# A scan's skip term as a diagonal matrix product, with its reader on another engine

## The reference, cut to what matters

```python
xc = silu(conv(x_ssm) + conv_b)                      # 4 x 512 x 256
dt = softplus(dt_r @ dt_proj_w.T + dt_proj_b)
dA = exp(dt[..., None] * A)
dBx = dt[..., None] * Bv[:, :, None, :] * xc[..., None]
h = dA_t * h + dBx_t                                 # for each step t
y = einsum('bdn,bn->bd', h, C_t)
y = ys + xc * D                                      # the skip term
return y * silu(z) @ out_proj_w.T
```

## Time and profile before

| | |
|---|---|
| median of 3 runs | 1700.42 us (1700.09 to 1701.14) |
| profiled execution | 1702.22 us |
| its span, first to last instruction | 1700.4 us |
| TensorE matmul busy | 1603.6 us (94%) |
| VectorE busy | 1213.6 us (71%) |
| ScalarE busy | 1046.0 us (62%) |
| GpSimd busy | 1014.2 us (60%) |
| mean granted clock of TensorE | 0.981 |

### The profile page before, as it was taken

How to read it: one execution, slowest core, us unless ns; L and a number is a source line. 1 busy time by engine, 2 the same in 40 slices (tenths; PEclk the granted TensorE clock), 3 DMA queues, 4 the chain that set the end, 5 groups by cost and what they waited for, 6 DMA issues and landing times.

```text
span 1700.4 us, 24061 instructions
## 1 busy us (share of the span) xinstructions
PE 1603.6 (94%) x7156; PEld 1225.9 (72%) x7156; DVE 1213.6 (71%) x2082; ACT 1046.0 (62%) x2093; POOL 1014.2 (60%) x976
## 2 busy tenths in 40 slices
PE   8999788788899999999899999998999999999998
PEld 6777444344577767877788778887887778878886
DVE  4565798889756656896678468876784588756665
ACT  4344867666443466676678666665785666656665
POOL 1100667767410068987333589883435788878887
PEclk8999899989999999999999999999999999999999
DMA  2000000000000066665000256652002567656664
GB/s 107 24 0 0 1 1 1 0 1 1 26 1 1 1 177 160 173 163 145 23 1 1 73 144 176 172 136 58 1 1 55 146 159 173 156 151 172 170 174 105
DMA packets 57829, 137.36 MB, mean 81 GB/s; under 512 B 10267, under 2 KB 33267, under 8 KB 57331
## 3 DMA queue, kind: packets, MB, share of 16 engines
q1 hardware_dynamic: 57715, 135.99, 31.0%
HBM read 133.86 MB, written 2.10 MB: 80 GB/s over the span
## 4 chain that ended last, share of the span: by engine, by line
PE 74%; POOL 8%; ACT 7%; issue 5%; DVE 3%; PEld 1%; PEldq 1%; POOLq 1%; DMA 0%; SPq 0%; ACTq 0%; DVEq 0%
PE ps L228 22%; PE ps L229 21%; PE ps L230 21%; POOL ln_c L1180 6%; PE ps L1706 2%; PE ps L905 1%; PE ps L1691 1%; PE ps L1692 1%; PE ps L1693 1%; POOL e_lo L236 1%; PE ps L371 1%; PEldq L217 1%; ACT ln_t L1017 1%; ACT L1017 1%; PE ps L377 1%
## 5 line engine op out<-in xcount | busy, mean ns | idle before, releaser
L236 POOL TENSOR_TENSOR e_lo<-e_h,e_hi 128x512 fp32r<-128x512 f32 (+1 forms) x368 | 476.6, 1295 | 128.2 <-ACT e_hi L233 117.4
L1356 ACT ACTIVATE e_s<-ps 128x512 f32<-128x512 f32 (+1 forms) x368 | 220.1, 598 | 267.8 <-PE ps L230 267.0
L1512 DVE TENSOR_TENSOR ps<-e_s,ps 128x512 f32<-128x512 f32 x352 | 244.8, 695 | 185.4 <-PE ps L230 150.6
L228 PE MATMUL ps<-xn_hi,eh 128*128 128x512 f32 x704 | 283.3, 402 | 9.1 <-ACT e_s L1356 7.4
L229 PE MATMUL ps<-xn_lo,eh 128*128 128x512 f32 x704 | 280.0, 398 | 0.0
L230 PE MATMUL ps<-xn_hi,el 128*128 128x512 f32 x704 | 279.3, 397 | 0.0
L1517 DVE TENSOR_TENSOR e_h<-ps,rwb 128x512 f32<-128x512 f32 x352 | 243.4, 691 | 14.8 <-DVE ps L1512 2.2
L236 POOL TENSOR_TENSOR el<-e_raw,eh 128x128 fp32r<-128x128 f32 (+1 forms) x352 | 219.8, 624 | 23.5 <-ACT eh L1345 23.5
L233 ACT ACTIVATE e_hi<-e_h 128x512 fp32r<-128x512 f32 (+1 forms) x368 | 229.5, 624 | 6.6 <-DVE e_h L1517 6.5
L1180 POOL TENSOR_TENSOR ln_c<-m_h,m_c 128x512 f32<-128x512 f32 x128 | 168.5, 1322 | 78.7 <-DVE m_h L1125 71.0
L228 PEld LDWEIGHTS ps<-xn_hi,eh 128*128 128x128 f32 x704 | 132.4, 188 | 49.5 <-ACT e_s L1356 10.0
(11 more groups left out here) (273 smaller groups left out, 3277.5 us busy)
## 6 DMA issues: line engine op xcount, KB each, us to landing
e_raw<-in_experts SPq DMA_DIRECT2D x176, 192.0 KB, 3.9
rwb<-rw_rows SPq DMA_DIRECT2D x64, 352.0 KB
rwb<-rw_rows SPq DMA_DIRECT2D x80, 256.0 KB
rwb<-rw_rows SPq DMA_DIRECT2D x32, 320.0 KB
rwb<-rw_rows SPq DMA_DIRECT2D x48, 192.0 KB
rwb<-rw_rows SPq DMA_DIRECT2D x32, 224.0 KB
rwb<-rw_rows SPq DMA_DIRECT2D x32, 160.0 KB
rwb<-rw_rows SPq DMA_DIRECT2D x80, 64.0 KB
```

What stands on the lines that cost most here:

```text
L228: pe.matmul(out, w_hi, x_hi, start=start, stop=False, skip_group_check=True)
L236: return eng.tensor_tensor(lo, full, hi.bitcast(F32), ALU.subtract)
L1356: act.activation(e_s[0:rows_, buf, :], ps[0:rows_, 4, :], ACT.Silu).then_inc(S["silu"], 1)
L1512: dve.tensor_tensor(ps[:, bank, :], e_s[:, buf, :], ps[:, 5, :], ALU.mult).then_inc(S["gated"], 1)
```

## The change

The skip term becomes a product on TensorE, with a diagonal matrix of D that VectorE makes once. It is the first of the sum, ahead of the identity product of state 0, so that one starts the bank and the other accumulates. VectorE's two additions are gone; ScalarE copies the sums from PSUM to `m_y` in `finish` of items 5 and 6. The steps that follow (gating, high and low part, output product, add) and those that use bank 6 after them come one item later.

```diff
+                skip_d = fb("skip_d", [P, MC, P])
...
-            for q in range(12):
+            for q in range(13):
                 finish(NB - 1, q)
...
-                    if q == 13:
+                    if q == 14:
                         ...
                         bc_proj(i + 1, FREE_BANK)
-                    if q == 17:
+                    if q == 18:
                         ...
                         dt_proj(i + 1, FREE_BANK)
...
                 if n == 0:
                     after(pe, "ylin", 2 * i + m - 1)
+                    pe.wait_ge(*M("skip_set", MC))
+                    pe.wait_ge(*M("xc", 2 * i + m + 1))
+                    pe.matmul(ps[:, 4 + m, :], skip_d[:, m, :], xc[:, i % 3, m, :], start=True, stop=False, skip_group_check=True)
                 pe.wait_ge(*M("hc", 32 * i + q + 1))
-                pe.matmul(ps[:, 4 + m, :], ident, m_hc[:, q % DEEP, :], start=(n == 0), stop=(n == DS - 1),
+                pe.matmul(ps[:, 4 + m, :], ident, m_hc[:, q % DEEP, :], start=False, stop=(n == DS - 1),
...
             def finish(i, q):                       # TensorE
-                if q == 9:
+                if q == 10:
...
-                    if q == 17:
+                    if q == 18:
                         bc_high(i + 1, FREE_BANK)
...
             def finish(i, q):                       # ScalarE
+                if q in (5, 6):
+                    m = q - 5
+                    act.wait_ge(*M("y_sum", 32 * i + 31 + m))
+                    after(act, "g_lo", 2 * i - 1 + m)
+                    act.activation(m_y[:, m, :], ps[:, 4 + m, :], ACT.Identity).then_inc(M["ylin"], 1)
-                if q == 9:
+                if q == 10:
...
+            for m in range(MC):                     # VectorE, once
+                dve.tensor_scalar(skip_d[:, m, :], ident, cols[:, C_D + m:C_D + m + 1], None, ALU.mult).then_inc(M["skip_set"], 1)
...
-                    if q == 16:
+                    if q == 17:
                         bc_low(i + 1, FREE_BANK)
...
             def finish(i, q):                       # VectorE
-                if q == 1:
-                    for m in range(MC):
-                        dve.wait_ge(*M("y_sum", 32 * i + 31 + m))
-                        dve.scalar_tensor_tensor(m_y[:, m, :], xc[:, i % 3, m, :], cols[:, C_D + m:C_D + m + 1], ps[:, 4 + m, :],
-                                                 ALU.mult, ALU.add).then_inc(M["ylin"], 1)
...
-                if q == 11:
+                if q == 12:
                     dve.wait_ge(*M("out", i + 1))
...
             def finish(i, q):                       # GpSimd
-                    if q in (2, 3):
+                    if q in (3, 4):
...
-                    if q in (7, 8):
+                    if q in (8, 9):
```

More of the change, by code:

```diff
@@ L207, in program @@
             "bcproj dtproj bc_hi bc_lo v vabs e ln dt du b_spread c_spread da db h c_copy hc y_sum ylin "
-            "gated g_hi g_lo out x_new aexp bc_zero").split(), 0), 1)
+            "skip_set gated g_hi g_lo out x_new aexp bc_zero").split(), 0), 1)
         A, = group("att", dict.fromkeys((
@@ L1193, in finish @@
                 if i < NB - 1:
-                    if q in (2, 3):
-                        m = q - 2
+                    if q in (3, 4):
+                        m = q - 3
                         pool.wait_ge(*M("sz", 2 * i + 2))
@@ L1198, in finish @@
                         pool.tensor_tensor(m_y[:, m, :], m_y[:, m, :], sz[:, i % 3, m, :], ALU.mult).then_inc(M["gated"], 1)
-                    if q in (7, 8):
-                        m = q - 7
+                    if q in (8, 9):
+                        m = q - 8
                         pool.wait_ge(*M("g_hi", 2 * i + m + 1))
```

## The result

The changed kernel takes 1705.78 us (median of 8 runs, 1704.39 to 1707.95), the kernel before 1699.72 (8 runs, 1695.16 to 1701.14): ratio 1.0037, 95% interval 1.0027 to 1.0047. It is slower, by some 6.1 us. Its profiled execution took 1707.95 us (span 1705.6, mean granted clock 0.980), 5.7 more than the one of before; each of the two is the slowest of its eight. Run again beside the last experiments (E9) it gave 1.0035 (1.0024 to 1.0045), with a second profiled execution of 1705.74 us.

What follows compares the result with a forecast made beforehand. VectorE was taken to set the scan phase's pace. Terms 0.4 + 2.0 + 2.0 - 0.6 + 1.3 - 0.65 = +4.45 took 1700.42 to 1704.9 us, range 1698.5 to 1708.5.

Steps and rivals of the forecast that it cites:

- The late read: Starts of blocks 1 to 3: TensorE waits 3.5, 3.5 and 2.75 us for ScalarE's read, queued behind the copy of C.
- Gain against new wait: Starts of blocks 1 and 2: 1.29 us saved by removed additions, against 1.4 us wait for spread 5 at full clock.
- full-clock replay: Starts of blocks 1 and 2 without half clock: spread 5 at 255.3, spread 6 at 258.0, nothing gained or lost.
- The half clock: TensorE at 1.2 GHz behind the new wait: +2.0 us each in blocks 1 and 2, bounds 0 and +2.5.
- block 3: Its start: new TensorE wait of 2.75 us, -0.1 at full clock, 0.7 to 1.7 later at half; taken as +1.3.
- rival B: Half clock behind the new wait in two of three blocks: about 1.9 us less, 1703.0; chance 0.20.
- six of six waits: All six earlier waits for the copy of C of 2.55 us or more went with TensorE at half speed.
- The moved steps: Output product and other steps one item later: -0.3 us in each of blocks 1 and 2, bounds 0 and -2.9.
- Rival D: Full clock at block starts and behind the shorter wait ahead of the output product: -6.15, 1694.3; chance 0.08.
- Block 0: Skip products add 1.7 to 2.6 us ahead of spread 6, against 1.31 cover: +0.4, bounds 0 and +1.3.
- The tail: End of the phase: with ScalarE reading instead of VectorE's second addition, the second gating ends earlier, -0.65 us.

Runs made afterwards that it cites:

- E9: The changed kernel run once more, nothing altered, against the kernel before; 1704.35 us, ratio 1.0035.
- E1: Changed kernel, but ScalarE reads the two sums in items 3 and 4 instead of 5 and 6; 1699.67 us, ratio 0.9996 to the kernel before.
- E4 short: Changed kernel plus 11 calls (22 small useless matmuls) on TensorE ahead of the wait for ScalarE's read, blocks 1 and 2; 1702.11 us, 1.0007 to before.
- E3: Changed kernel without the skip product (D * xc left out of the result), ScalarE still reading late; 1699.42 us, ratio 0.9997 to the kernel before.
- E2: Kernel before, VectorE's additions kept and no skip product, but the later steps one item later as in the change; 1699.38 us, ratio 1.0000.
- E5: Changed kernel with ScalarE reading in items 3 and 4 and later steps in their old items, skip product first; 1697.27 us, 0.9993 to before.
- E7: Kernel before with only ScalarE's reads in items 3 and 4 and the skip product ahead of products 6 and 7; 1693.41 us, 0.9961, again 0.9976.
- E8: Changed kernel with the skip product ahead of products 6 and 7 instead of 0 and 1, read still late; 1696.56 us, ratio 0.9978 to before.

## Why the prediction was right

The forecast, slower at 1704.9, and the range held, and the median moved by 6.1 us where 4.45 were forecast. The mechanism held for blocks 1 and 2, which carry 3.6 us of it; that the rest of the sum came out near is in part luck. Step by step:

**The late read.** Predicted waits of TensorE 3.5, 3.5 and 2.75 us; measured 3.50, 3.50 and 2.73. The replay of ScalarE's queue (exponential, copy of C that waits for GpSimd, then the read) was exact, since none of its links depends on the change. E1 shows that the place of the read decides: about 7 us.

**Gain against new wait.** VectorE's wait for spread 5 was put at 3 us at half clock and 1.4 at full: 3.10 and 3.07 in the change, 1.43 in E4 short. Up to scan 11 each of the two blocks lost 1.8 us where I took 2.0, and 0.1 in E4 short where the full-clock replay said 0.

**The half clock.** Right for blocks 1 and 2, wrong for block 3: in the clock this is rival B, which was priced at 1703.0. The step that failed is the rule taken from six of six waits, that a wait in this range is always followed by 1.2 GHz. In block 3 the wait of 2.73 us is followed by 2.4 GHz in both profiles of the change; E3 has 2.4 GHz behind 3.50 us in block 2 and mostly 1.2 behind 2.75 us in block 3. The wait's length alone doesn't decide. (The prediction's remark that by the length alone the clock would have stayed full has no row behind it: in the profile of before all six waits of 2.55 us or more ended or were followed by half clock.) The Trainium skill (TensorE: Matmul & The Clock Gate, What's actually happening) says of the monitor that it sets the clock by "how busy the PE has been recently"; E4 short agrees, which at the same read keeps 2.4 GHz by filling the wait. What was over by 1.45 us in the sum is this term; the full-clock figure of the prediction for block 3, -0.1, is what came (-0.15).

**The moved steps.** Priced at -0.3 a block, measured -0.15 and +0.49, together 0.9 off; E2, and E1 against E5, give zero within 3 us. The replay at half clock was right: from TensorE's restart at 270.15, spread 13 is used at +3.0 us, the add starts at +6.7 (predicted +6.8), scan 13 at +7.9 (predicted +8.0). Rival D, the clock staying up behind a shorter wait ahead of the output product, did not come in the change (wait 3.60 us, then 1.2 GHz), but it is what happens in one of E7's two profiled executions, behind 2.87 us.

**Block 0 and the tail.** The tail came as forecast, -0.56 against -0.65. Block 0's +0.61 against +0.4 is luck: it is two waits of 1.35 us in all, 1.57 by the scans and so above the bound of 1.3, less 1 us that scans 12 to 18 took longer, at a lower clock, in the profile of before. In E9 the waits don't come at all (0.07 us).

**What was missing.** 1.83 us at items 20 to 22 of block 3, in a stretch that I didn't look at because no edited line runs there. Two misses (block 3 too dear by 1.45, moved steps too cheap by 0.94) and this one add to 1.3 us, so the time came out near partly by cancelling. Why the clock falls there is open.

**What the prediction didn't separate.** It named ScalarE's place as the cause and counted the product as a term of the same chain. E1 and E3 show that neither costs what can be told without the other: together 6 us lost, with either undone 0.7 and 0.5 us below the kernel before, which can't be told from it. E8 shows the same a third way, with both in place but the product three states later: 0.9978, below the kernel before.

## What to carry to other kernels

When work is moved to another engine, the price isn't its busy time there but what stands ahead of it in that engine's queue: here a copy that waits for a third engine; two items earlier no such wait stood ahead of it. Here only the first term of the accumulation waited for the bank, so the extra term did better in the middle, just ahead of a wait that TensorE had anyway. Follow the whole kernel behind a changed clock history, also where no line was edited. And profile a kernel twice before a difference of 1 to 3 us between two traces is put down to the change: here one stretch of block 0 gave +0.6 and -2.3 us for the same program.

## What the runs showed of the hardware

- Full clock after a long wait: in E3 TensorE did nothing for 3.50 us and then came from the product's start to the next spread's in 0.56 us (320.24 to 320.80), while behind the same wait in block 1 it took 1.08 us (250.06 to 251.14).
- In E4 short, behind 22 small matmuls (128 x 128, 2.72 us in all) in the wait for the read, the clock was 2.4 GHz, in both blocks; 48 of them took 5.62 us and overran the wait.
- Two profiled executions of the changed kernel, same program: mean granted clock 0.86 and 1.00 in the same 12 us of block 0, and 0.72 in the profile of before.
- VectorE's plain copies of the two sums take 1.26 us, where its additions with D took 1.39.
